# A top-k search for eight experts: from a bitwise search on float scores to a two-half search on whole-number keys, with a third of the counting on ScalarE

## The reference, cut to what matters

```
capacity = max(1, int(CAPACITY_FACTOR * n / e))      # 4096 rows, 8 experts: 512
scores = (x_flat @ Wg.T).T                           # 8 x 4096
top_vals, token_idx = jax.lax.top_k(scores, capacity)
token_w = jax.nn.softmax(top_vals, axis=-1)
xg = x_flat[token_idx]
...
out = jnp.zeros_like(x_flat).at[token_idx.reshape(-1)].add(y.reshape(-1, c))
```

## Time and profile before

| what | value |
|---|---|
| median of 3 runs | 718.16 us (717.76 to 723.28) |
| span of the profiled execution | 713.3 us |
| outside the span, median less span | 4.86 us |
| DVE busy over the whole span | 426.9 us, 60% |
| PE busy over the whole span | 518.2 us, 73% |
| ACT busy over the whole span | 332.8 us, 47% |

### The profile page before, as it was taken

The page is one execution under the profiler, slowest core; times in us unless marked ns, Lnnn a source line. Parts: engine busy times, 40 slices in busy tenths (PEclk is TensorE's granted clock), DMA queues, the critical chain, the costliest instruction groups (busy, mean ns, idle before and its releaser), DMA issues.

```text
span 713.3 us, 13599 instructions
## 1 busy us (share of the span) xinstructions
PE 518.2 (73%) x3894; PEld 382.3 (54%) x3896; DVE 426.9 (60%) x1784; ACT 332.8 (47%) x690; POOL 313.0 (44%) x329
## 2 busy tenths in 40 slices
PE   1769610378777508877899997149999999999925
PEld 1457100245544303433334444149999999999921
DVE  4789668835322238898426878883545545455447
ACT  3815510044323115454357663165666666666616
POOL 3514300067878723243001112016777667767535
PEclk9966755569978758899999998559999999999976
DMA  7401272012323350100000100021111111111155
GB/s 189 130 0 56 69 291 123 6 38 41 45 43 43 34 173 28 31 15 1 2 0 16 31 27 20 15 24 42 50 48 49 46 47 48 48 44 49 38 202 167
DMA packets 47736, 42.23 MB, mean 59 GB/s; under 512 B 15346, under 2 KB 41835, under 8 KB 47179
## 3 DMA queue, kind: packets, MB, share of 16 engines
q1 hardware_dynamic: 35770, 25.48, 11.4%
q0 software_dynamic: 10816, 15.82, 10.6%
q10 hardware_dynamic: 1104, 0.39, 0.2%
HBM read 26.23 MB, written 15.30 MB: 58 GB/s over the span
## 4 chain that ended last, share of the span: by engine, by line
PE 45%; DVE 27%; issue 11%; POOL 6%; ACT 5%; DMA 4%; ACTq 1%; DVEq 0%; POOLq 0%; SPq 0%
PE bank L1886 18%; PE bank L1907 9%; DVE st L1259 3%; POOL sum_dram L673 3%; PE bank L1695 2%; PE bank L1740 2%; PE bank L1730 2%; DVE mv L1264 2%; POOL arena L661 2%; DVE st L989 2%; ACT arena L913 1%; POOL rstd L687 1%; PE bank L1796 1%; DVE hit L1103 1%; PE bank L1896 1%
## 5 line engine op out<-in xcount | busy, mean ns | idle before, releaser
L1886 PE MATMUL bank<-arena 128*128 128x128 f32 x1136 | 140.1, 277 | 0.4 <-ACT arena L964 0.4
L1886 PEld LDWEIGHTS bank<-arena 128*128 128x128 f32 x1136 | 133.9, 194 | 0.7 <-ACT arena L964 0.7
L687 POOL TENSOR_TENSOR rstd<-ve,mhalf 128x4 f32<-128x4 f32 x40 | 48.7, 1217 | 167.7 <-DVE ve L1267 121.7
L1519 DVE TENSOR_TENSOR arena<-arena,bank 128x512 f32<-128x512 f32 x71 | 48.8, 688 | 81.4 <-PE bank L1886 81.4
L741 POOL DMA_INDIRECT y_dram<-arena,sidx x71 | 69.9, 985 | 44.4 <-DVE arena L1524 41.1
L950 ACT ACTIVATE arena<-wgu 128x1024 f32 x71 | 75.0, 1057 | 26.5 <-PE bank L1886 26.2
L733 POOL DMA_INDIRECT arena<-x3row_dram,gidx x71 | 68.8, 969 | 36.5 <-issue 20.7
L1907 PE MATMUL bank<-w,arena 128*128 x568 | 75.1, 275 | 0.0
L1907 PEld LDWEIGHTS bank<-w,arena 128*128 128x128 f32 x568 | 69.1, 192 | 0.2 <-issue 0.2
L956 ACT ACTIVATE arena<-bank 128x512 f32<-128x512 f32 x71 | 42.4, 597 | 42.7 <-PE bank L1886 42.7
L673 POOL DMA_INDIRECT sum_dram<-arena,idx x32 | 50.7, 1585 | 15.2 <-issue 7.6
(11 more groups left out here) (326 smaller groups left out, 1049.0 us busy)
## 6 DMA issues: line engine op xcount, KB each, us to landing
wgu<-in_wgu SPq DMA_DIRECT2D x1, 4096.0 KB, 12.2
wgu<-y_dram SPq DMA_DIRECT2D x8, 512.0 KB, 6.7
X<-in_x SPq DMA_DIRECT2D x8, 256.0 KB, 5.6
sum_dram<-zero POOLq DMA_DIRECT2D x8, 256.0 KB, 4.2
x1row_dram<-row SPq DMA_DIRECT2D x8, 256.0 KB, 2.4
w<-in_w SPq DMA_DIRECT2D x1, 2048.0 KB, 17.4
acc<-sum_dram SPq DMA_DIRECT2D x8, 256.0 KB, 2.9
w<-in_wd SPq DMA_DIRECT2D x1, 2048.0 KB, 10.2
```

What stands on the lines that cost most here:

```text
L687: nc.gpsimd.tensor_tensor(out, ve[:, u], mhalf[:, 0:J], ALU.pow).then_inc(done, 1)
L1519: nc.vector.tensor_tensor(gl[:, m.pair], sgl[:, m.pair], bank[3 + m.pair][:], ALU.mult).then_inc(f_gated, 1)
L1886: last = nc.tensor.matmul(bank[first + m.pair][:, h * P:(h + 1) * P], wnow[:, m.pair, at_:at_ + P], xrT[:, m.ring], start=True, stop=True)
```

## The change

The scores are first turned into whole numbers that sort as the scores do: the word of a float, with all bits but the sign turned where the sign is set, read as a signed integer. The search runs in two halves. The first eight rounds look for the upper 16 bits of the last score, the next eight for the lower 16 bits among numbers in which the upper part is already subtracted (scaled by 2^-16). Both halves work on float tiles `key[:, 0]` and `key[:, 1]`, which hold these numbers.

- A round still has three thresholds. DVE counts two of them (L1131, "less than"), ACT counts the third: `Sign` of threshold less key, with a sum of the signs over the columns (L825). The third threshold lies half a step off, so that no sign is zero.
- PE adds the counts onto a bank into which it has already added the required number with a minus sign (`needed`, L1644), so a threshold is met where the sum is at most zero. This first matmul of round r+1 is issued right behind the second matmul of round r, into the other of two banks.
- DVE turns the three sums into the rise of the threshold in one instruction (L1154, product with the round's `unit` and a sum), and adds that to the four words of `cand` in one more (L1163). The fixed part of the next thresholds was added before, behind the counts (L1137).
- The keys of the first half are made ahead of the first round (L1124 to L1126). The lower half's key is made in rounds 4, 5 and 6 behind the counts (L1148, L1150, L1152) and completed between rounds 7 and 8 (L1158, L1160). The largest score is found in round 0 behind the counts (L1139), spread in rounds 2 and 3.
- There are 16 rounds, and no first and last round of one threshold.

The diff, cut to its core:

```
-ROUNDS = 15
+ROUNDS = 16
+HALF_WAY = ROUNDS // 2
...
+            for r in range(ROUNDS):
+                act.wait_ge(c_cnt, LEAD + 2 * r + 2)
+                with nc.allow_low_precision("whole numbers up to 256"):
+                    nc.scalar.activation(slots[:], key[:, 0 if r < HALF_WAY else 1], ACT.Sign, bias=cand[:, r % 2, 2:3], scale=-1.0,
+                                         accum_out=cntb[:, 2:3]).then_inc(c_act, 1)
+                if r == 2:
+                    act.wait_ge(r_wr, LEAD + 1)
+                    nc.scalar.activation(wr_mean[:], bank[0][:, 0:E1], ACT.Copy, scale=-1.0 / D).then_inc(r_wr, 1)
...
-            ch.mark(nc.vector.memset(step[:], 0))
-            ch.wait()
+            nc.vector.tensor_copy(cand[:, 0], moves[:, 0])
             dve.wait_ge(a_scst, LEAD + SCORES * CH)
-            count(step[:], cntb[:, 0:1], hit).then_inc(c_cnt, 1)
-            nc.vector.tensor_reduce(cg[:, 3:4], srch[:], AX.X, ALU.max).then_inc(c_mx, 1)
...
+            do(nc.vector.tensor_scalar(qi[:, 0], bits, 31, 0x7fff, ALU.arith_shift_right, ALU.bitwise_and))
+            do(nc.vector.scalar_tensor_tensor(qi[:, 1], bits, 16, qi[:, 0], ALU.arith_shift_right, ALU.bitwise_xor))
+            nc.vector.tensor_copy(key[:, 0], qi[:, 1]).then_inc(c_cnt, 1)
             for r in range(ROUNDS):
                 at = r % 2
-                for q, junk in enumerate((hit, eq, rank)):
-                    last = count(cand[:, at, q + 1:q + 2], cntb[:, q:q + 1], junk)
-                last.then_inc(c_cnt, 1)
...
-                dve.wait_ge(c_tot, LEAD + r + 2)
-                ch.mark(nc.vector.tensor_scalar(met[:, 0:3], total[:, 0:3], float(CAP), None, ALU.is_ge, ALU.add,
-                                                accum_out=met[:, 3:4]))
-                ch.wait()
-                ch.mark(nc.vector.tensor_scalar(step[:], met[:, 3:4], low_bit[:, r:r + 1], None, ALU.mult))
-                ch.wait()
-                ch.mark(nc.vector.scalar_tensor_tensor(cand[:, 1 - at], bits[:, r + 1], step[:],
-                                                       cand[:, at, 0:1].to_broadcast([P, 4]), ALU.bitwise_xor,
-                                                       ALU.bitwise_xor))
-                ch.wait()
+                dve.wait_ge(c_cnt, LEAD + 2 * r + 2)
+                for q, junk in enumerate((hit, eq)):
+                    counted = nc.vector.tensor_scalar(junk[:], key[:, 0 if r < HALF_WAY else 1], cand[:, at, q:q + 1], None,
+                                                      ALU.is_lt, ALU.add, accum_out=cntb[:, q:q + 1])
+                counted.then_inc(c_cnt, 1)
+                if r == HALF_WAY - 1:
+                    nc.vector.tensor_copy(cand[:, 1 - at], moves[:, HALF_WAY])
+                elif r < ROUNDS - 1:
+                    ch.mark(nc.vector.tensor_tensor(cand[:, 1 - at], cand[:, at], moves[:, r + 1], ALU.add))
+                if r == 0:
+                    nc.vector.tensor_reduce(cg[:, 3:4], srch[:], AX.X, ALU.max).then_inc(c_mx, 1)
...
+                if r == 5:
+                    ch.mark(nc.vector.scalar_tensor_tensor(qi[:, 1], bits, 0xffff, qi[:, 0], ALU.bitwise_and, ALU.bitwise_xor))
+                if r == 6:
+                    ch.mark(nc.vector.tensor_scalar(key[:, 1], qi[:, 1], 2.0 ** -16, None, ALU.mult))
+                dve.wait_ge(c_tot, LEAD + r + 1)
+                do(nc.vector.scalar_tensor_tensor(met[:, 0:3], total[at][:, 0:3], 0.0, unit[:, r:r + 1].to_broadcast([P, 3]),
+                                                  ALU.is_le, ALU.mult, accum_out=rise[:, at:at + 1]))
+                if r == HALF_WAY - 1 or r == ROUNDS - 1:
+                    half = r // HALF_WAY
+                    do(nc.vector.tensor_tensor(lowest[:, half:half + 1], cand[:, at, 3:4], rise[:, at:at + 1], ALU.add))
+                    if half == 0:
+                        nc.vector.scalar_tensor_tensor(key[:, 1], key[:, 0], lowest[:, 0:1], key[:, 1], ALU.subtract,
+                                                       ALU.add).then_inc(c_cnt, 1)
+                else:
+                    nc.vector.tensor_scalar(cand[:, 1 - at], cand[:, 1 - at], rise[:, at:at + 1], None, ALU.add).then_inc(c_cnt, 1)
...
             for r in range(ROUNDS):
-                total(r + 1, 3)
-                if r == 2:
+                pe.wait_ge(c_cnt, LEAD + 2 * r + 3)
+                pe.wait_ge(c_act, LEAD + r + 1)
+                nc.tensor.matmul(bank[(7, 2)[r % 2]][:, 0:3], blk_b[:], cntb[:, 0:3], start=False, stop=True).then_inc(c_tot, 1)
+                if r < ROUNDS - 1:
+                    start_total(r + 1)
```

More of the change, by code:

```diff
@@ L174, in program @@
         qi = sb("qi", [P, 2, SEG], I32)
-        qf = sb("qf", [P, 2, SEG])
         slots = sb("slots", [P, SEG])
-        cand = sb("cand", [P, 2, 4], U32)
-        step = sb("step", [P, 1], U32)
-        cntb = sb("cntb", [P, 3], BF16)
+        cand = sb("cand", [P, 2, 4])
+        rise = sb("rise", [P, 2])
+        cntb = sb("cntb", [P, 4], BF16)
+        needed = sb("needed", [P, 4], BF16)
+        lowest = sb("lowest", [P, 2])
         cgb = sb("cgb", [P, 2], BF16)
@@ L1096, in _, with do @@
             dve.wait_ge(s_later, LEAD + 16 * len(LATER))
-            total = bank[7]
-            def count(thr, out, junk):
-                return nc.vector.tensor_scalar(junk[:], srch[:], thr.bitcast(F32), None, ALU.is_ge, ALU.add, accum_out=out)
+            total = (bank[7], bank[2])
+            bits = srch[:].bitcast(I32)
+            def do(ins):
+                ch.mark(ins)
+                ch.wait()
             ch.begin(0, 0)
@@ L1144, in _ @@
-                ch.wait()
-            count(cand[:, 1, 1:2], cntb[:, 0:1], hit).then_inc(c_cnt, 1)
-            dve.wait_ge(c_tot, LEAD + ROUNDS + 2)
-            ch.mark(nc.vector.tensor_scalar(step[:], total[:, 0:1], float(CAP), None, ALU.is_ge))
-            ch.wait()
-            ch.mark(nc.vector.tensor_tensor(cand[:, 0, 0:1], cand[:, 1, 0:1], step[:], ALU.bitwise_xor))
-            ch.wait()
-            thr = cand[:, 0, 0:1].bitcast(F32)
-            nc.vector.tensor_scalar(sel[:], srch[:], thr, None, ALU.is_gt, ALU.add, accum_out=cgb[:, 0:1])
@@ L1155, in _ @@
+            thr = lowest[:, 1:2]
+            nc.vector.tensor_scalar(sel[:], key[:, 1], thr, None, ALU.is_gt, ALU.add, accum_out=cgb[:, 0:1])
+            nc.vector.tensor_scalar(eq[:], key[:, 1], thr, None, ALU.is_equal, ALU.add,
                                     accum_out=cgb[:, 1:2]).then_inc(c_post, 1)
@@ L1920, in _, with search_moves @@
             each_group(add_choices, 0)
+def search_moves():
+    moves, unit, base, before = [], [], 0.0, None
+    for r in range(ROUNDS):
+        half, k = divmod(r, HALF_WAY)
+        scale = 2.0 ** (-16 * half)
+        u = scale * 4.0 ** (HALF_WAY - 1 - k)
+        off = np.array([u, 2 * u, 3 * u - scale / 2, 0.0])
+        moves.append(off - before if k else off - (32768.0 if half == 0 else 0.0))
+        unit.append(u)
+        before = off
+    return np.array(moves, np.float32), np.array(unit, np.float32)
 def kernel(**inputs):
@@ L1975 @@
     form_pair[0, 32] = 1
+    moves, unit = search_moves()
     arrays = {
@@ L1988 @@
         "tri": np.kron(np.eye(E0), np.triu(np.ones((16, 16)), 1)).astype(np.float32),
-        "bits": np.repeat(np.array([[[0, 1 << low, 2 << low, 3 << low] for low in range(29, 0, -2)] + [[0, 1, 0, 0]]],
-                                   np.uint32), P, axis=0),
-        "low_bit": np.repeat(2.0 ** np.arange(29, 0, -2, dtype=np.float32)[None], P, axis=0),
+        "moves": np.repeat(moves[None], P, axis=0),
+        "unit": np.repeat(unit[None], P, axis=0),
         "quad": np.tile(np.kron(np.eye(4), np.ones((1, 4))), (P // 4, 1)).astype(np.float32),
```

64 lines of the change are left out of this document (31 added, 33 removed).

## The result

The changed kernel takes 710.9 us (median of 4 runs, 709.55 to 711.19), beside 718.94 us for the kernel before, run with it (4 runs, 717.76 to 723.28). The ratio is 0.9887, with an interval of 0.9844 to 0.9929. The forecast was 709.3 us, in a range from 707.3 to 712.2.

A forecast was written before the change was run, and what follows sets the result against it. Bound: the search, a single dependent loop mostly on DVE. 1.15 + 16 x 1.63 + 0.20 + 0.47 - 0.05 = 27.85 us against 36.72, so 718.16 - 8.87 = 709.3 us, range 707.3 to 712.2.

The forecast's parts named there:

- The round: Plain search round, first count to first count: 0.41 + 0.54 + 0.23 + 0.20 + 0.25 = 1.63 us, sixteen times.
- The rival with a dear `met`: Three-operand step after PE's sum takes 0.34, not 0.20, adding 2.2 us: 711.5 us; chance 0.07.
- ScalarE: ACT's third count, threshold to PE: done after some 0.78 us, 0.17 before DVE, costing nothing.
- the late one: ACT's sum read-out is a second pass, 0.16 a round, 2.6 us: 711.9 us; chance 0.09.
- the table load: A 1.283 us load ahead of every ACT sign, 1.09 more each round: 726.7 us; chance 0.03.
- The opening, the middle and the end: Key making before round 0: 1.15 us; between rounds 7 and 8: 0.47 more; behind round 15: 0.05 less.
- What is put behind the counts: Extra DVE instructions in the 0.37 us free each round, behind the second count: 0.20 us in all.
- its sign that rounds 0 and 5 would be longer by about a tenth: In the changed profile, the rounds with the maximum and the lower key's three-operand step would grow about a tenth.
- The rule on three-operand steps: Half rate for two non-bf16 sources would add 0.27 us to each of three DVE steps; not followed, 0.485 kept.
- All of it reaches the end: Everything behind the search moves up, so its 8.87 us come off the whole time: 718.16 to 709.3 us.
- The rival in which half of the gain is lost behind the search: Experiments' rival: 4 to 5 us gained. The prediction's version, gain lost behind the search: about 718 us, chance 0.04.
- The time outside the span: The 4.86 us by which the runs' median exceeds the profiled span of 713.3 us, taken as unchanged.

The follow-up runs named there:

- the copy: Changed kernel with ACT also copying the keys into an unused tile before each sign: 712.41 us, ratio 0.9897.
- the rise within the counts: Changed kernel with DVE's counts comparing key less last rise with a threshold made a round earlier: 707.1 us, ratio 0.9865; again 707.35 us, 0.9878.
- half of the search: Changed kernel running only rounds 0 to 7, the lower 16 bits left out: 697.07 us, ratio 0.9696.
- the waiting step: Changed kernel with one more dependent one-column DVE instruction per round, its result unread: 714.43 us, ratio 0.9951.

## Why the prediction was right

**The round.** Forecast 1.63 us, measured 1.64. Term by term, measured (forecast): count to count 0.41 (0.41), second count to PE's load 0.53 (0.54), load to `met` 0.23 (0.23), `met` to the last step 0.21 (0.20), last step to the next count 0.26 (0.25). The forecast took every term but one from a row of the same or a near shape in the kernel before, and so missed by a hundredth.

**`met`.** That one is the three-operand `met` with a sum, bounded by 0.16 and 0.34 and taken at 0.20, the value of the two-operand one. It was 0.21 to the next instruction. The rival with a dear `met` falls.

**ScalarE.** Forecast: done 0.78 us after the threshold, hand-overs included, 0.17 ahead of DVE. Measured: the read-out begins 0.42 after the sign, takes 0.19, and where ACT was made to be last (the copy) PE's load came 0.11 behind it: 0.72, against DVE's 0.94. The read was sized well (0.171 taken, 0.188 measured); the forecast counted the sign's whole 0.51 and took the hand-over to PE at 0.05. The two errors nearly cancel, and the slack is some 0.22, as the copy shows. Both rivals on ScalarE fall, the late one and the table load: between the signs the trace has no load (ACT's 35 instructions in the search are 16 signs, 16 reads and the three that were there before).

**The opening, the middle and the end.** The opening took 1.12 us (forecast 1.15). Its three-operand step on integers took 0.42, not 0.485, and the conversion 0.29 (0.285). The middle, from the first count of round 7 to that of round 8, took 2.08 us, 0.44 more than a plain round (forecast 0.47). The last round took 1.57, 0.07 less than a plain one (forecast 0.05). That the whole search came out within 0.05 us of the 27.85 is luck in part: the rounds are 0.16 longer in all, the other terms together some 0.2 shorter.

**What is put behind the counts.** Forecast 0.20 in all. Rounds 0, 5 and 6 took 1.67, 1.68 and 1.65 us: 0.03, 0.04 and 0.01 over a plain one. The forecast named the right rounds and took more than twice what they cost; its sign that rounds 0 and 5 would be longer by about a tenth did not come.

**The rule on three-operand steps.** The forecast kept the row of 485 ns against the Trainium skill's rule, "Vector Engine (DVE) Microarchitecture Reference", section "Points that are easy to get wrong". No halving shows: 0.42 on integers, 0.48 for the lower keys, and in the version with the rise within the counts 28 such counts with a sum, this group of DVE's and its twin (columns as in the earlier trace rows):

```profile
L1142 DVE SCALAR_TENSOR_TENSOR hit<-key,rise,cand 128x256 f32<-128x256 f32 x14 | 6.8, 485 | 0.5
L1142 DVE SCALAR_TENSOR_TENSOR eq<-key,rise,cand 128x256 f32<-128x256 f32 x14 | 6.7, 481 | 0.0
```

Their second tensor is one column stretched over 256; the lower keys' step has two full tensors, but no sum. Two full fp32 tensors together with a sum were not run.

**All of it reaches the end.** This was the step with the least evidence: the chain showed only the store ahead of the first gather. Across six kernels the search and the median move together, taken from the second measurement of the changed kernel: 6.41 and 6.49 us with the third count on DVE, -13.56 and -14.17 with half of the search, 1.29 and 1.17 with the copy, and 8.92 and 8.93 for the kernel before; from another chip, where the kernel before was 2.4 us lower too, 3.00 and 3.19 with the waiting step, -2.15 and -4.1 with the rise within the counts. Three of these carry the reading, since their runs do not overlap those of the changed kernel beside them (710.57 to 712.94): the kernel before (715.58 to 723.73), the third count on DVE (713.69 to 721.14) and half of the search (696.12 to 698.77). The rival in which half of the gain is lost behind the search would have needed about 3 and 7 us in the last two, not 6.5 and 14.2. The agreement to a tenth of a microsecond is luck, with runs this far apart, and the small steps do not show by themselves. That the one profiled pair of spans shows 4.3 us goes in part with the clock in the rows above, for whose drift the forecast allowed 1.8 us either way; runs of the kernel before differ by more than that among themselves, and the clock was not varied apart.

**What was mis-sized.** The time outside the span. The forecast took it as 4.86 us, the median of the runs less the span of one profiled execution. In every run that lists both, it is 1.8 to 2.2 us (here 710.79 - 709.0 = 1.79). The profiled execution of the kernel before would therefore have taken some 715.2 us, near the lower end of that kernel's runs (713.5 to 723.7 on all chips). The forecast did not hang on the term, since it was left unchanged on both sides; but the median it was subtracted from did move. Medians of the kernel before were 717.8 to 720.2 on different occasions. The gain of 8.87 against the 718.94 measured beside the changed kernel gives 710.1, and the 0.8 that is left lies inside the runs' spread. The gain in time is 8.0 us by the medians of one measurement and 8.9 by the other (8.1 and 7.6 by their ratios), and the intervals don't part these.

## What to carry to other kernels

In a loop where every instruction waits for the one before, a round can be priced closely from rows of the same shape (here to a hundredth of a microsecond), and the profit is the sum over the rounds: one count of 0.40 moved to an idle engine was worth 6.4 us, one waiting step of a few columns about 0.2 us each time. Before work goes to an idle engine, add up its whole branch from the common release to the common consumer, read-out and hand-overs included; what is left over is the room for more (here 0.22 us, and a one-column sum of 0.29 used it up). To learn what a stage is worth to the end, lengthen and shorten the stage itself, and compare medians: the spans of two single profiles can be off by half the gain.

## What was not expected of the hardware

- ACT's read-out of a sum is a row of its own, 188 ns, and starts before the recorded end of the sign: 0.42 after a start whose row has 0.51. Likewise a copy of 0.42 delayed the sign behind it by 0.32.
- ACT's instruction on one column with two operands from SBUF took 0.29 us, more than the 0.171 of the one-column copy from PSUM in the earlier trace rows, and more than POOL's 0.19 for the same sum. The Trainium skill, "ScalarE: Activation LUTs", section "What ACT_TABLE_LOAD costs", gives an instruction with a pointer bias about 280 ns and 0.83 ns for each column, and lets instructions back to back overlap by some 93 ns; the traces agree with both (0.29 for one column, and 0.10 between the copy of 0.42 and the sign 0.32 behind its start).
- DVE's count beside POOL's one-column addition took 0.51, not 0.48, in thirteen of fourteen rounds (0.48 in round 1, where POOL's addition took 0.43). The Trainium skill, "GPSIMD Engine Reference", section "1. Specifications", says that the two engines share their SBUF interfaces and contend where a DVE instruction has two SBUF inputs, as this count has (the second a stretched column); the 30 ns would be its price here, but it was not tried by itself.
- The runs of the kernel before differ by up to 10 us, and the longer ones mostly have the lower mean granted clock (723.69 us at 0.837, 715.58 at 0.849 on one chip); the ten runs of the changed kernel differ by 3.4 at most (709.55 to 712.94). In the profiles of all these kernels two stages differ in length: the experts' first one, in which the clock rises late, early, or falls back, with 105.4 to 108.4 us from the first gather to the last scatter, and the linear-attention layer, with 83.5 to 86.4 us from the first to the last start of the ACT group named above. One and the same kernel has both 86.3 and 85.1 us there (the rise within the counts, in its two profiles), so the lengths vary without a change of the kernel. What decides them stays open.
